# A feed-forward stage whose quantising, scaling and weight squarings are put on other engines and in other places

## The reference, cut to what matters

```python
def activation_quant(x):
    s = 127 / clip(max(abs(x), axis=-1), 1e-5)
    return clip(round(x * s), -128, 127) / s
def bit_linear(x, w):                  # weight_quant: w to -1, 0, 1 times its mean size
    return einsum('bsh,oh->bso', activation_quant(x), weight_quant(w))
# feed-forward, layer 0, on the layer-normed x
h = silu(bit_linear(x, w_gate)) * bit_linear(x, w_up)
h = rms_norm(h, ln_weight)             # ln_weight * h * rsqrt(mean(h*h) + 1e-6)
x = x + bit_linear(h, w_down)
# scan, layer 1, on the layer-normed x
dt = softplus(Wdt(dt_x) + bdt);  dA = exp(dt * A);  dBx = dt * B * x
state = dA * state + dBx;        y = (state * C).sum() + x * D
x = x + y
```

## Time and profile before

| quantity | value |
| --- | --- |
| median of three runs | 1124.81 us (1124.12 to 1127.18) |
| the profiled execution's own time | 1126.66 us |
| its span in the trace | 1124.9 us |
| busy: PE / DVE / ACT / POOL | 85% / 70% / 57% / 47% |
| feed-forward stage, from the norm of x to its last sum | 188.3 to 258.2 us |
| start of the scan, up to its regular steps | 258.2 to 288.9 us |
| the granted TensorE clock, mean of the span | 0.93 |

### The profile page before, as it was taken

How to read it: one execution, slowest core, us unless ns; L and a number is a source line. 1 busy time by engine, 2 the same in 40 slices (tenths; PEclk the granted TensorE clock), 3 DMA queues, 4 the chain that set the end, 5 groups by cost and what they waited for, 6 DMA issues and landing times.

```text
span 1124.9 us, 15437 instructions
## 1 busy us (share of the span) xinstructions
PE 959.0 (85%) x5202; PEld 602.3 (54%) x5218; DVE 789.0 (70%) x1301; ACT 640.8 (57%) x1509; POOL 528.6 (47%) x392
## 2 busy tenths in 40 slices
PE   5888796555566775698899999999989999999998
PEld 3666543232122223466677777777765665555554
DVE  4578798878999997787888777788775354333233
ACT  2655495677888735777877767777663332111111
POOL 4222363441899923587777665776654222000000
PEclk9899897868789787899999999999999999999999
DMA  9634002300000000000000422000030000000000
GB/s 336 286 130 150 1 1 85 92 0 1 0 1 0 0 1 0 1 1 2 1 1 1 124 63 74 1 1 2 2 112 20 1 1 1 1 20 1 1 1 20
DMA packets 24223, 43.13 MB, mean 38 GB/s; under 512 B 3600, under 2 KB 19920, under 8 KB 22608
## 3 DMA queue, kind: packets, MB, share of 16 engines
q1 hardware_dynamic: 24144, 42.14, 11.0%
HBM read 41.08 MB, written 1.05 MB: 37 GB/s over the span
## 4 chain that ended last, share of the span: by engine, by line
PE 59%; DVE 15%; POOL 9%; issue 8%; ACT 8%; DMA 0%; DVEq 0%; ACTq 0%; SPq 0%; POOLq 0%
PE ps L2329 13%; PE ps L2350 9%; PE ps L1901 4%; PE ps L1914 4%; PE ps L1860 4%; PE ps L1868 3%; PE ps L1885 3%; ACT ps L2174 3%; POOL wide L1404 3%; POOL arena L1247 3%; PE ps L1893 2%; PE ps L1875 2%; PE ps L2339 2%; PE ps L445 2%; PE ps L485 1%
## 5 line engine op out<-in xcount | busy, mean ns | idle before, releaser
L2368 DVE TENSOR_TENSOR arena<-arena,ps 128x512 f32<-128x512 f32 (+1 forms) x56 | 38.5, 688 | 146.0 <-ACT arena L2361 143.9
L2361 ACT ACTIVATE arena<-ps,arena 128x512 f32<-128x512 f32 (+1 forms) x56 | 38.4, 686 | 156.0 <-PE ps L2329 156.0
L2253 POOL TENSOR_TENSOR arena<-arena 128x4 f32<-128x4 f32 x96 | 98.8, 1030 | 50.8 <-DVE arena L2025 48.2
L2350 PE MATMUL ps<-wide,arena 128*128 128x256 f32 (+1 forms) x448 | 106.3, 380 | 0.0
L2174 ACT ACTIVATE ps<-ps,arena 128x128 f32<-128x128 f32 x256 | 88.4, 355 | 29.0 <-DVE arena L2004 29.0
L2166 ACT ACTIVATE arena<-ps,ones 128x512 f32<-128x512 f32 x96 | 68.1, 786 | 61.0 <-PE ps L1875 61.0
L2350 PEld LDWEIGHTS ps<-wide,arena 128*128 128x128 f32 (+1 forms) x448 | 84.7, 190 | 17.9 <-issue 1.8
L2329 PE MATMUL ps<-XT,wide 128*128 128x512 f16 (+1 forms) x384 | 93.3, 379 | 0.0
L2004 DVE TENSOR_REDUCE arena<-ps 128x4 f32<-128x512 f32 x64 | 43.7, 689 | 53.8 <-PE ps L1885 53.7
L1868 PE MATMUL ps<-wide,arena 128*128 128x512 f16 x256 | 67.5, 400 | 13.6 <-ACT arena L2166 7.1
L1202 PE MATMUL ps<-arena,ident 128*128 128x512 f32 x128 | 73.0, 725 | 1.9 <-POOL arena L1247 1.9
(11 more groups left out here) (347 smaller groups left out, 2403.7 us busy)
## 6 DMA issues: line engine op xcount, KB each, us to landing
side<-in_wproj SPq DMA_DIRECT2D x1, 4096.0 KB, 16.8
wide<-in_w_down SPq DMA_DIRECT2D x1, 3584.0 KB, 13.7
side<-in_w_gate SPq DMA_DIRECT2D x1, 3520.0 KB, 18.7
side<-in_w_up SPq DMA_DIRECT2D x1, 3520.0 KB, 12.4
wide<-in_w_gate SPq DMA_DIRECT2D x2, 1728.0 KB, 12.1
side<-in_w_up SPq DMA_DIRECT2D x3, 1024.0 KB, 9.1
arena<-in_taps SPq DMA_DIRECT2D x1, 2048.0 KB, 10.9
wide<-in_wq SPq DMA_DIRECT2D x1, 2048.0 KB, 18.5
```

The source lines that it names most:

```text
L2253: pool.tensor_tensor(rs[:, j, :], var[:, j, :], minus_half[:, j, :], ALU.pow).then_inc(rs_ready, 1)
L2350: last = pe.matmul(self.out(b), self.hid[n % 2][0:m, b * S:(b + 1) * S], self.down[0:m, j, :], start=(j == 0 and b % 2 == 0), stop=(j == M ...
```

## The change

- The last six batches are normalised on VectorE (`norm_apply`), as the first two are. `offset` and ScalarE's writing of XN are gone. `steps` for these six batches comes ahead of the loop.
- Quantising x: VectorE does batches 0 and 1, ScalarE the other six (`quantise_x`, two instructions for each batch, between the copy of the next batch and the square).
- The first `down_steps` serves five batches instead of six, and stands, with the scaling of batches 0 and 1, ahead of the last `multiply` instead of behind all of them. ScalarE takes the constant off for all batches. Scaling runs four batches ahead instead of three.
- The first last-stage product waits for seven products of the loop instead of eight.
- Squarings 12 and 13 stand one turn of the loop earlier. Squarings 14 and 15 are no longer in the feed-forward stage but on ScalarE in the scan stage, behind the four copies of the turned norm and ahead of the copies of the low-rank rows.

```diff
         def front(b):
+            dve.wait_ge(steps_ready, 1)
             wait(dve, xq_ready, b)
-            link(dve.tensor_scalar(xi, k.XN[:, b, :], aq[:, b:b + 1], ROUND, ALU.mult, ALU.add))
-            wait(dve, xqT_psum, b - 1)
-            dve.tensor_scalar(xq[b % 2], xi, -ROUND, None, ALU.add).then_inc(xq_ready, 1)
+            link(dve.tensor_scalar(xi[0], k.XN[:, b, :], aq[:, b:b + 1], ROUND, ALU.mult, ALU.add))
+            dve.tensor_scalar(xq[b % 2], xi[0], -ROUND, None, ALU.add).then_inc(xq_ready, 1)
...
-        dve.wait_ge(k.std_ready, 6)
-        link(dve.reciprocal(k.rstd[:, 2:B], k.std[:, 2:B]))
-        dve.scalar_tensor_tensor(offset[:, 2:B], k.mv[:, 2:B, 0], -1.0, k.rstd[:, 2:B], ALU.mult,
-                                 ALU.mult).then_inc(offset_ready, 1)
+        k.norm_apply(dve, link, 5, k.X, range(2, B))
+        steps(2, B - 2)
         for b in range(B):
-            if b and b + 2 < B:
-                front(b + 2)
+            if b == B - 1:
+                link(last)
+                down_steps(0, 0, FIRST)
+                scale(0)
+                scale(1)
             multiply(b)
             if b:
                 last = biggest(b - 1)
-            if b == 0:
-                steps(2, B - 2)
-                front(2)
         link(last)
-        down_steps(0, 0, FIRST)
-        quantise(0)
-        quantise(1)
+        scale(2)
         link(biggest(B - 1))
-        scale(2)
+        scale(3)
         down_steps(1, FIRST, B)
...
+        def quantise_x(b):
+            act.wait_ge(steps_ready, 2)
+            wait(act, xq_ready, b)
+            link(act.activation(xi[1], k.XN[:, b, :], ACT.Copy, scale=aq[:, b:b + 1], bias=ROUND))
+            act.wait_ge(xqT_psum, b - 1)
+            act.activation(xq[b % 2], xi[1], ACT.Copy, bias=-ROUND).then_inc(xq_ready, 1)
...
             if b + 1 < B:
                 front(b + 1)
+            if b + 2 < B:
+                quantise_x(b + 2)
             if b:
                 square(b - 1)
-            if b in (4, 6):
+            if b in (3, 5):
                 act.wait_ge(sq_done, b)
-                k.proj.square(act, 10 + b // 2, k.junk)
-                act.wait_ge(k.proj.squared, 11 + b // 2)
+                k.proj.square(act, 12 + b // 4, k.junk)
+                act.wait_ge(k.proj.squared, 13 + b // 4)
+        rounded(0)
+        rounded(1)
+        turned(0)
         square(B - 1)
-        act.wait_ge(sq_done, B)
         for b in range(B):
-            turned(b)
+            if b:
+                turned(b)
             if b + 2 < B:
                 rounded(b + 2)
-            if b < 2:
-                k.proj.square(act, 14 + b, k.junk)
...
         k.turn_scalar(act, 2)
+        for i in range(14, 16):
+            w.square(act, i, k.junk)
         for j in range(2):
             act.wait_ge(low_psum, j + 1)
```

More of the change, by code:

```diff
@@ L745, in ffn @@
     lnw = A.take([FF])
-    xi = A.take([D])
+    xi = [A.take([D]) for _ in range(2)]
     sg = A.take([FF])
@@ L752, in ffn @@
     hqT = [A.take([FC, P], BF16) for _ in range(2)]
-    small = A.take([14, B])
+    small = A.take([13, B])
     k.junk = A.take([2048], BF16)
     assert A.at <= 15360, A.at
-    amax, ainv, aq, gstep, ustep, ss, hmax, hms, hr, hstep, hq_scale, dstep, minus_half, offset = (
-        small[:, i, :] for i in range(14))
+    amax, ainv, aq, gstep, ustep, ss, hmax, hms, hr, hstep, hq_scale, dstep, minus_half = (
+        small[:, i, :] for i in range(13))
     gate, up, down = k.ternary
     GATE, UP = (4, 0), (6, 2)
-    FIRST = 6
+    FIRST = 5
     lnw_loaded = k.sem("ff_lnw_loaded")
     steps_ready = k.sem("ff_steps_ready")
-    offset_ready = k.sem("ff_offset_ready")
     xq_ready = k.sem("ff_xq_ready")
@@ L902, in rounded @@
             act.wait_ge(hq_scaled, b + 1)
-            act.wait_ge(hqT_psum, b - 1)
+            wait(act, hqT_psum, b - 1)
             act.activation(hq[b % 2], h[b], ACT.Copy, bias=-ROUND).then_inc(hq_ready, 1)
@@ L909, in scalar @@
         front(0)
-        act.wait_ge(offset_ready, 1)
-        for b in range(2, B):
-            act.activation(k.XN[:, b, :], k.X[:, b, :], ACT.Identity, scale=k.rstd[:, b:b + 1],
-                           bias=offset[:, b:b + 1]).then_inc(k.xn_ready, 1)
         for b in range(B):
```

18 lines of the change are left out of this document (6 added, 12 removed).

## The result

The changed kernel takes 1129.03 us (median of 18 runs), the kernel before 1125.14 in its 18 runs beside them. The ratio is 1.003, with a 95% interval of 1.0019 to 1.0041: the change costs 3.9 us. The forecast was 4.5. That the changed kernel is slower is clear, since the interval lies above 1. Whether it is more than 0.3% slower, the line that the prediction drew for "no change", the interval can't tell: 1.003 lies on it.

The account below looks back on a forecast made before the run. No engine was full throughout: VectorE bound the gate and up loop, ScalarE and TensorE in turn the last product. Median 1124.81, less 8.8, plus 13.3 gave 1129.3, rounded to 1129.4; 8-in-10 range 1122.4 to 1133.5.

Parts of the forecast that it names:

- the up product: Start of the stage: four matmuls of the up product at the low clock take 1.75 us before the second product.
- part 1: Start of the feed-forward stage: norms go to VectorE, ScalarE quantises batch 2; second product near 202.9, 3.9 us gained.
- TensorE's clock: Last product: three turns at the low clock, 2.56 us each, then ScalarE's pace; gain 8.8 us.
- part 3: Turn into the last product and that product: down steps earlier, two squarings gone; last sum at 248.5, gain 8.8 us.
- Part 2: Loop over gate and up products: ScalarE becomes limit, 3.5 us a turn against 4.11; nothing added to part 1's gain.
- Rival B: Last product at low TensorE clock throughout, or ScalarE's loop turn 4.1 us: gain only 5.3, time 1132.8; chance 0.2.
- Part 4: Scan's start: two squarings there make the factors late, VectorE waits; delay 13.3 us, bounds 11 and 14.
- a little might come back: Scan's start: table load falling into the wait and earlier GpSimd splitting lower the delay from 13.9 to 13.3 us.
- Rival A: Scan's start: the 7.1 us behind the reduction not paid again; 1122.4 us, not slower; chance 0.13 with a related form.
- Rival C: Whole kernel: gain 9.9 and loss 11.5, both a little better than reckoned; 1126.4 us, no measurable change; chance 0.17.

Follow-up runs that it names:

- E1: Changed kernel with squarings 14 and 15 put back into the last product, none in the scan: ratio 0.9942 to the kernel before, 1119.53 us.
- E2: Kernel before with only squarings 14 and 15 moved to the scan: ratio 1.0093 to the kernel before, 1136.85 us.
- E9: Changed kernel with VectorE, not ScalarE, quantising x of batches 2 to 7, ahead of each product: ratio 1.0028 to the kernel before, 1129.47 us.
- E6: Changed kernel with VectorE, not ScalarE, quantising x of batches 2 to 7, behind each product: ratio 1.0118 to the kernel before, 1139.52 us.
- E12: E11 with squaring 15 moved behind ScalarE's two low-rank copies: ratio 0.9933 to the kernel before, 1118.81 us.
- E5: Changed kernel with GpSimd's reduction over the partitions replaced by a copy: ratio 0.9964 to the kernel before, 1121.95 us.
- E3: Changed kernel with VectorE's constants moved from the scan's start to ahead of its fifth step: ratio 1.0005 to the kernel before, 1126.85 us.
- E4: Changed kernel with squarings 14 and 15 in ScalarE's gaps of the feed-forward stage, none in the scan: ratio 0.9923 to the kernel before, 1117.28 us.
- E11: Changed kernel with VectorE's constants moved behind the scan's loop, squarings 14 and 15 still in the scan: ratio 0.9951 to the kernel before, 1121.17 us.
- E10: E4 with VectorE, not ScalarE, quantising x of batches 2 to 7, ahead of each product: ratio 0.9931 to the kernel before, 1118.76 us.

## Why the prediction was right, step by step

The time was 1129.03 us, the forecast 1129.4. The mechanism was right on both sides: a feed-forward stage that gets shorter, and a wait of VectorE for the factors that costs more. E1 and E2 show each half alone, and they add. Both halves were sized too small, by 3.0 and 1.8 us, and most of that cancelled. The closeness of the total is in part luck. Two terms within the gain had the wrong reason as well: the up product in part 1, and TensorE's clock in part 3.

**Part 1, start of the stage.** Forecast 3.9 us, measured 4.7. The first product came 11.15 us into the stage, as forecast (11.1). The second followed 2.6 us behind it where the sum had 3.5. Its rows, TensorE's and then ScalarE's and VectorE's:

```profile
204.34 1.03 PE L941 MATMUL ps<-arena 128*128 128x512 bf16 x4
204.47 1.11 ACT L883 ACTIVATE arena<-ps,arena 128x1024 f32<-128x1024 f32 x1 [0.32 <-DVE XT L813]
205.69 1.28 DVE L813 SCALAR_TENSOR_TENSOR XT<-ps,arena 128x1024 f32<-128x1024 f32 x1 [1.33 <-ACT arena L883]
```

Four matmuls of the up product took 1.03 us where the sum had 1.75 at the low clock: that is most of the miss, and the rest is turning and quantising (1.1, measured 0.96 here and 0.87 in the loop). The up product was there at 205.37. So the second product did not wait for the chain that the sum followed, by a little, but for silu, which had waited for the first product (0.32). E9 came to 15.7 for this product with VectorE's quantising in place of 13.8, so some 2.8 of the 4.7 us are the norms and `steps` ahead of the loop.

**Part 2, the loop.** Forecast 3.5 us a turn, measured 3.16, with ScalarE as the limit: 0.87 of quantising for 1.1, and 2.29 of its other work for 2.42. A turn with a squaring is 2.18 longer, forecast 2.1. The silu of batch 7 was expected 36.6 us into the stage and started at 35.3.

**Part 3, turn and last product.** The down steps behind GpSimd's work took 1.29, and the last product of the loop started 39.8 us into the stage where 41.5 was expected. The third scaling beside GpSimd ended at 44.0 for 45.8. Forecast and trace have the exclusion between a VectorE instruction from and to SBUF and a GpSimd one: 1.82 us for one scaling, 1.42 for two. The Trainium skill, "SBUF — State Buffer", Who interferes with whom, states this, and the rows agree, E6 (2.31) and E9 (1.53) too. The first down product came at 42.5, expected at 43.8. From there to the last sum were 15.1 us where the gain of 8.8 allowed 16.8. The forecast put a term for the clock there, three turns at the low level, and in this trace only the first down product ran slow (1.57, then 1.05). But the clock is not what made the difference. E12 has the same feed-forward stage, and in its trace three down products ran slow (TensorE):

```profile
230.46 1.89 PE L973 MATMUL ps<-arena 128*128 128x256 bf16 x8 [0.16 <-ACT arena L893]
234.05 1.89 PE L973 MATMUL ps<-arena 128*128 128x256 bf16 x8
236.59 1.44 PE L973 MATMUL ps<-arena 128*128 128x256 bf16 x8
```

Its last sum still comes 57.8 us into the stage, for 57.6 here, and 15.2 us behind the first down product, for 15.1. In both traces ScalarE has no gap from the third rounding on and takes some 1.86 us a batch, where the forecast had 1.95 and let TensorE's 2.56 be the slower of the two for three turns. So the mis-sized term is this one: ScalarE set the pace throughout. Why the clock rises when it does stays open, since it differs in equal code. What the traces show is what TensorE did before: in E1, with the squarings back, its turning of batch 2 had run at the high level (eight transposes in 0.62 us), then it waited 2.17 us for ScalarE, and the next eight matmuls took 1.89. Rival B's first form, a low clock throughout, is false, and so is its second, a turn of 4.1 us on ScalarE. The gain was 11.8, not 8.8. Of the 3.0 us of the miss, 1.8 were there when the third scaling ended, and 1.2 arose behind it; 0.4 of these the forecast had taken off itself, from 9.2 to 8.8.

**Part 4, the scan's start.** The forecast's chain held link by link: two squarings, 4 us; the reduction with its gap; GpSimd's small work; the constants; L1077. The loss was 15.1 us for 13.3. Of the 1.8 us, 0.7 are the turning of the norm (its last copy ended 6.4 us behind the last sum, before 5.65), where sixteen transposes of L177 took 3.42 us for 2.70, at a granted clock of 0.74 (250 to 256.5 us) for 1.00 (258.2 to 264 before), and 0.5 are the gap behind the reduction (8.07 from start to start for 7.59). The other 0.6 had been taken off because a little might come back, and nothing did: the second L1077 takes 3.08 as before. The idle time of L1795 was expected at 15 to 17 us and is 17.5, longer by the first two of these terms. Rival A, that the 7.1 us aren't paid again, is false by the trace (7.56) and by E5 (8.0 us less on the path without the reduction).

**Rival C** had the gain of 9.9 with a loss of 11.5. It was right on the side of the gain and wrong on the other.

What stays open: why the granted clock, ahead of the stage and within it, differs between executions of equal code, and what of E3's 8 us was rhythm.

## What to carry to other kernels

When work is moved out of a crowded stage, ask who waits for its result and what is queued in that engine's order behind the waiting instruction; here 4.6 us were gained, and 17.5 us of VectorE were lost to constants that no instruction reads before 431.6 us in the trace, some 158 us later. Cheaper than moving work out is to move it into a gap of the same stage (1.6 us for two squarings in E4, though that left the factors a slack of 0.1 us) or to move the waiting instruction down (E11), and the spot within a rhythm matters as much as the stage (E3 against E11, E6 against E9). Compare traces from a common mark ahead of the change, not from the span.

## What the runs showed of the hardware

- Ahead of the stage, executions of equal code ended 187.6 to 191.9 us after the span's start; with a start at 188.3 (before) the granted clock of 30 to 60 us was 0.93, with one at 191.9 (after) 0.82. The two don't go together strictly: E10 had 0.83 there and was 1.5 us behind the trace of before at 117 us, but 0.1 ahead of it at 139, and its stage began at 188.4.
- The first GpSimd instruction behind PARTITION_ALL_REDUCE starts 7.59 us (before) and 8.07 us (after) after it, whose own record has 0.51; behind a plain copy it is 0.28 (E5). A switch of GpSimd's configuration stands at the gap's start in both (246.9 us in the earlier trace rows, 260.4 after); that the switch is its cause is not isolated. Ahead of the reduction there is a switch too, and in E4 the reduction started 5.7 us behind it although all sums were there; in the kernels before and after it lay within the wait for the 16th sum.
- Two VectorE products of 128x8 elements took 1.52 and 2.16 us beside GpSimd's work (E3) and 0.17 and 0.16 without it: next to GpSimd's work their size did not tell their time.
- The same VectorE quantising gives a turn of 4.11 us ahead of the product that releases GpSimd (E9) and 6.09 behind it (E6).
